# Pieces of two long filters, spread in another way over the four batches of a delta rule

## What is computed

```python
q = silu(dwconv(x @ q_w.T)); k = ...; v = ...          # 4 heads of 64 channels
beta = sigmoid(x @ b_w.T)
# delta rule, per head, in chunks of the sequence
inv = solve_triangular(eye + A, eye, lower=True)       # A = strictly lower part of (k*beta) @ k.T
u = inv @ v; w = inv @ kb
u_adj = u_i - w_i @ S; o_i = q_i @ S + attn @ u_adj; S = S + k_i.T @ u_adj
short, long_, wide = fir(v, 3 taps), fir(v, 31 taps), fir(v, 64 taps)   # causal, one filter a channel
gate_in = concat(x, stats(short), stats(long_), stats(wide), stats(delta_out), stats(v))
o = w0*short + w1*long_ + w2*wide + w3*delta_out + w4*v
```

## Time and profile before

| | |
|---|---|
| median of 3 runs | 709.68 us (709.62 to 709.91) |
| the profiled execution | 705.24 us |
| its span, first to last instruction | 703.4 us |
| busy, share of the span | PE 83%, PEld 61%, DVE 65%, ACT 40%, POOL 17% |
| mean granted clock of TensorE | 0.944 of full |

### The profile page before, as it was taken

How to read it: one execution, slowest core, us unless ns; L and a number is a source line. 1 busy time by engine, 2 the same in 40 slices (tenths; PEclk the granted TensorE clock), 3 DMA queues, 4 the chain that set the end, 5 groups by cost and what they waited for, 6 DMA issues and landing times. The chain is left out here.

```text
span 703.4 us, 16960 instructions
## 1 busy us (share of the span) xinstructions
PE 585.3 (83%) x7436; PEld 426.2 (61%) x7448; DVE 455.5 (65%) x890; ACT 282.8 (40%) x518; POOL 118.5 (17%) x102
## 2 busy tenths in 40 slices
PE   5868679899998999878696886599999767998984
PEld 2544466777767676776443545488888554555542
DVE  2963367857784786774818889664277774676674
ACT  1874634432453344323344253332323144554431
POOL 1001340250034006000011203434100020000000
PEclk9999899999999999998799998899999887999998
DMA  5501420340052004001510005400000000000001
GB/s 175 207 1 44 152 79 4 104 139 4 4 156 89 3 23 161 4 4 64 207 31 30 31 0 156 134 1 0 1 1 0 1 0 1 1 0 31 31 4 58
DMA packets 26537, 37.51 MB, mean 53 GB/s; under 512 B 4641, under 2 KB 13602, under 8 KB 26463
## 3 DMA queue, kind: packets, MB, share of 16 engines
q1 hardware_dynamic: 26463, 36.42, 16.0%
HBM read 34.31 MB, written 2.10 MB: 52 GB/s over the span
## 5 line engine op out<-in xcount | busy, mean ns | idle before, releaser
L298 DVE SCALAR_TENSOR_TENSOR arena<-bank,conv_w,arena 128x511 f32<-128x511 f32 (+2 forms) x72 | 53.2, 746 | 30.9 <-ACT arena L1070 15.5
L1448 POOL COPY arena<-v_win 128x256 f32<-128x256 f32 x32 | 21.1, 684 | 196.8 <-PE bank L732 196.8
L1898 ACT COPY arena<-bank 128x512 f32<-128x512 f32 x40 | 23.3, 584 | 57.1 <-PE bank L1701 36.8
L1701 PE MATMUL bank<-v_win,arena 128*128 128x256 f32 x192 | 45.6, 386 | 0.0
L2473 PE MATMUL bank<-v_win,arena 128*128 128x256 bf16 x288 | 36.5, 279 | 7.9 <-DVE arena L2560 6.9
L732 PE MATMUL bank<-arena 128*32 128x128 f32 x512 | 35.7, 409 | 8.1 <-ACT arena L1081 7.6
L1131 ACT COPY arena<-bank 128x512 f32<-128x512 f32 x40 | 21.6, 589 | 50.8 <-PE bank L854 50.8
L1086 ACT COPY arena<-bank 128x256 f32<-128x256 f32 x32 | 19.3, 602 | 53.9 <-PE bank L745 53.9
L1701 PEld LDWEIGHTS bank<-v_win,arena 128*128 128x128 f32 x192 | 37.1, 195 | 5.5 <-issue 0.4
L2473 PEld LDWEIGHTS bank<-v_win,arena 128*128 128x128 bf16 x288 | 28.4, 100 | 16.6 <-DVE arena L2560 7.9
L2463 PE MATMUL bank<-arena,v_win 128*128 128x512 bf16 x134 | 35.1, 390 | 3.7 <-DVE arena L2531 3.2
(11 more groups left out here) (275 smaller groups left out, 1355.4 us busy)
## 6 DMA issues: line engine op xcount, KB each, us to landing
arena<-in_toep_w SPq DMA_DIRECT2D x32, 256.0 KB, 3.0
arena<-in_toep_l SPq DMA_DIRECT2D x32, 256.0 KB, 3.7
arena<-in_xT SPq DMA_DIRECT2D x12, 512.0 KB, 4.6
arena<-in_x SPq DMA_DIRECT2D x4, 512.0 KB, 3.9
arena<-in_ctx SPq DMA_DIRECT2D x4, 512.0 KB, 4.4
out<-arena SPq DMA_DIRECT2D x4, 512.0 KB, 2.9
qkv_w<-in_qkv_wT SPq DMA_DIRECT2D x1, 768.0 KB, 5.4
v_win<-in_w_gateT SPq DMA_DIRECT2D x1, 768.0 KB, 4.9
```

The costliest lines, as they stand in the source:

```text
L298: return nc.vector.scalar_tensor_tensor(out=acc[:, j:L], in0=src[:, 0:L - j], scalar=conv_w[:, m, CONV_K - 1 - j:CONV_K - j], in1=acc[:, j:L],
L1701: i = mm(oo, src[:, k, f * P:(f + 1) * P], w[:, k, :], start=(k == 0), stop=(k == KT - 1 and f > 0))
L1898: nc.scalar.copy(dst(i), bank[RING_FIRST + n % RING].rearrange("p (t c) -> p t c", c=dst(i).shape[-1]))\
```

## The change

The recurrences of batches 0 and 1 get six pieces each in place of seven, that of batch 2 gets five, and pieces 25 to 28 go to the inverse of batch 3, one each at k = 2 to 5, where a batch with a successor has its projections. Their last turn stands where the next batch's `beta` would. The last recurrence keeps pieces 29 to 31. The work is the same; DVE's list does not change.

```diff
-        OPENING, PER_ROUND = 8, 7
-        pieces_of = lambda b: range(OPENING + b * PER_ROUND, min(OPENING + (b + 1) * PER_ROUND, NPIECE))
+        OPENING = 8
+        FIRST_OF, LAST_LEVELS = (8, 14, 20, 29, NPIECE), range(25, 29)
+        pieces_of = lambda b: range(FIRST_OF[b], LAST_LEVELS[0] if b == B - 2 else FIRST_OF[b + 1])
...
+                    if b == B - 1:
+                        for n in LAST_LEVELS:
+                            next_toep(n)
...
-                        pe.wait_ge(s2["fir_out"].sem, pieces_of(b)[0])
+                        pe.wait_ge(s2["fir_out"].sem, pieces_of(b - 1).stop if b else OPENING)
...
+                        else:
+                            if k == 2:
+                                pe.wait_ge(s2["attn_out"].sem, s2["attn_out"].at(b, 4))
+                            filter_piece(LAST_LEVELS[k - 2], first=(k == 2))
                         products_w(b, k, 0)
...
+                    else:
+                        to_tokens(LAST_LEVELS[-1])
                     corner(b, 0)
...
-                    if more:
+                    if last == 5:
                         filter_piece(piece[5])
 
                     state_part(b, 3)
-                    if more:
-                        filter_piece(piece[6])
                     updates(b, 3, more)
...
-                        to_tokens(piece[6])
+                        to_tokens(piece[last])
...
+                        if not more and k >= 2:
+                            filter_out(LAST_LEVELS[k - 2], first=(k == 2))
...
-                        copy_piece(piece[-1] + 1)
-                        copy_piece(piece[-1] + 2)
+                        for n in range(piece[-1] + 1, FIRST_OF[b + 1] + 2):
+                            copy_piece(n)
```

More of the change, by code:

```diff
@@ L974, in recurrence @@
                     piece = list(pieces_of(b))
+                    last = len(piece) - 1
                     if more:
@@ L1150, in inverse @@
                         beta_tanh(b + 1)
+                    else:
+                        tokens_out(LAST_LEVELS[-1])
                 def u_out(b, t):
@@ L1180, in recurrence @@
                         k_back_out(b + 1, 0, 1)
-                        filter_out(piece[5])
-                        filter_out(piece[6])
+                        for n in piece[5:]:
+                            filter_out(n)
                     else:
@@ L1187, in recurrence @@
                         cross_out(b + 1, 0)
-                        tokens_out(piece[6])
+                        tokens_out(piece[-1])
                         cross_out(b + 1, 1)
```

## The result

| | before | after |
|---|---|---|
| median of 4 runs each, same chip | 709.65 us (709.34 to 709.91) | 700.23 us (699.04 to 700.49) |
| ratio, 95% interval | | 0.9864 [0.9847, 0.9881] |
| the profiled execution | 705.24 us | 700.49 us |
| its span | 703.4 us | 698.7 us |

The account below looks back on a forecast made before the run. PE was taken to set the pace, with late code blocks and half clock in the last inverse. Recurrences -6.17 us and last inverse +1.6 us gave -4.6, so 709.68 became 705.1 us, range 701.8 to 707.8.

Parts of the forecast that it names:

- The recurrences: Recurrences of batches 0 to 2: removing pieces saves 1.50, 1.50 and 3.17 us, together 6.17 us.
- The Gram products: Gram products of batches 0 and 1: issue waits of 1.03 and 0.73 us, taken as staying in the sum.
- a rival from it for the worse alone: Gram products of batches 0 and 1: waits grow, each batch saves 1.0 us instead of 1.5; 706.1 us.
- The last inverse: Batch 3's inverse: four added pieces cost +1.6 us, the middle between -0.4 (none shows) and +3.6 (code blocks at batch 2's pace).
- Rival 2: Last inverse: levels run at batch 2's pace of code blocks, one in 4.62 us, +3.6 us; 707.1 us, chance 0.20.
- the inverse of batch 1: Batch 1's inverse: the forecast sum had no term for it.
- added its difference to the median: Whole kernel: median lies 4.4 us above the profiled execution, difference taken as unchanged, so -4.6 was applied to 709.68 us.
- Rival 1: Last inverse and Gram products: everything hidden and both Gram waits go, -8.3 us in all; 701.4 us, chance 0.13.
- Rival 3: Last inverse: each code block takes 5.29 us, +7.8 there, sum +1.6, a slower kernel; 711.3 us, chance 0.07.
- rival 4: Last recurrence at half clock: up to 3.9 us more could go; shifts each case by +-1.5 us; no chance of its own.

Follow-up runs that it names:

- the padded kernels: The kernel before with 64 or 128 instructions of unread 64x64 products added on PE in the opening; 0.9901 and 0.9924 of the kernel before.
- the two later comparisons: The changed kernel, unchanged, run again beside the kernel before, twice; 0.9891 (700.58 us against 707.67) and 0.9888 (699.85 us against 706.67).
- the control with 256: The kernel before with a whole block of 256 unread instructions (64 products of 64x64) added in the opening; 1.0051 of the kernel before.
- the pairs with equal padding: Kernel before and changed kernel, each with the same unread instructions in the opening: 0.9901 and 0.9918 with 64, 0.9924 and 0.992 with 128.
- two pieces: Against the changed kernel, two pieces instead of four in the last inverse, 7, 7 and 5 in the recurrences; 0.9915 of the kernel before.
- before again: The kernel before, unchanged, profiled and timed once more beside itself; 0.9979 of itself.
- removal alone: Against the changed kernel, pieces 25 to 28 left out altogether, nothing in the last inverse; 0.9855 of the kernel before, 697.81 us.

## Why the prediction was wrong

**The recurrences: right.** A clean recurrence with seven pieces takes 28.2 us, as the padded kernels show; after the change they are 26.7, 26.7 and 24.9. That is 1.5 + 1.5 + 3.3, where 1.50 + 1.50 + 3.17 were forecast.

**The Gram products: the first step that failed.** The sum took their two issue waits as staying, although had a price for them, and gave their going only to a rival. They went. The recurrence of batch 0 lost 2.7 and 2.0 us against the two profiles of before, that of batch 1 2.4: in the mean 1.7 us more than the pieces give. That these waits stand at borders of blocks is shown by the counts and the packets; the prediction had even said that the borders move by a piece's 64 instructions and drew a rival from it for the worse alone.

**The last inverse: the second step that failed, a right length from a wrong base.** The term was +1.6 us, on a base of 33.4. The changed stretch is 34.6 to 34.9 us, and the base is 33.5 in one profile and 35.9 in the other, so the measured term is +1.3 or -1.2, about nothing in the mean. But the pieces are not hidden. Against the same inverse without late blocks, 30.6 us, they cost 4.2 us: from level 2 to the end of `corner` 26.9 against 22.6 us (290.99 to 311.54 + 2.06 in the kernel with 64 instructions more). The prediction had 25.1 us for this without late code. Of the 1.8 us above it 0.6 are issue waits (0.26 and 0.38); the rest is spread over the levels (5.02 for 4.94) and the products behind them. It looked free since the base wasted 3 to 5 us. Rival 2's 29.1 us, a block each 4.62 us, did not come either: a block took 4.3.

**A term at nothing: the inverse of batch 1.** It takes 35.4, 35.5 and 34.5 us in the three profiles of the changed kernel against 34.47, since a block is late there in two of them (0.43 and 0.29 us, at different levels). That is +0.7 in the mean. The prediction had moved borders in mind, but not here.

**Summed up.** -4.6 as forecast, -1.7 for the Gram products, -1.6 for the inverse and +0.7 for batch 1's inverse give -7.2 us; stage 2 is 7.2 us shorter in the mean of the profiles (287.5, and 280.3 over three). The medians of the two later comparisons differ by 7.1 and 6.8 us. This is half as much again as forecast.

**The other 2 us.** The first comparison has 9.4 us. Its four executions of the kernel before have a median of 709.65 us, where the four later sets (11 to 29 executions each) have 706.7 to 707.7; the changed kernel has 700.2, 700.6 and 699.9. So the surplus lies on the side of the kernel before, in those four executions, and its cause stays open. The prediction, made against one execution 4.4 us under this median, added its difference to the median. That step did no harm: the two profiles of the kernel before differ by 3.0 us, 2.9 of them ahead of stage 2, where both kernels run the same code. What a single profile could not tell was how its last inverse and last recurrence share their half clock.

**The rivals.** Rival 1 came nearest in time (701.4), and half of its mechanism held, the waits in the Gram products; that everything is hidden in the last inverse did not. Rival 3, a slower kernel by late blocks, did not come; its mechanism was real but was in the kernel before. The clock (rival 4) moved 2.5 us in the base's last inverse and 1.7 us the other way in the recurrence behind it. The Trainium skill's page "Runtime: NRT & Kernel Launch", section "Instruction fetch mechanics", has blocks of 256 instructions, and the control with 256 and the places of all 36 waits bear that out. It has the cost of crossing a border as mostly hidden. By number of borders that holds, 36 waits at 681 of them; by time it fails here, since these few and the half clock behind them make most of the 7 us between good and bad borders in stage 2.

**What the change is worth.** The kernel before with 64 unread instructions is at 0.9901 [0.987, 0.9931], the changed kernel at 0.9864 to 0.9891. The later two comparisons of the changed kernel can't be told from it. Most of the gain is code that comes in time; moving pieces from the recurrences (6.3 us) to the last inverse (4.2 us) leaves at most 2 us, and in the pairs with equal padding nothing measurable. No kernel tried that does all the work was clearly faster than the changed one.

## What to carry to other kernels

Before costing a move of work, list the waits marked issue and count the instructions between them. When they are a block apart, look up when the packets of the instruction queue start, and ask what a shift of the borders would do, for the better as well as for the worse. A kernel with a few unread instructions more is the control without which a gain is put down to the wrong cause; check what the padding itself does to the time and the clock, and do not expect a whole block more to bring every wait back. Price a stretch against its clean length, not against one that carries a late block. And take a second profile of the kernel before, and compare stage by stage, before reading a gain off one pair of totals.

## What the runs showed of the hardware

- PE's code came in blocks of 256 instructions. In 18 profiles PE crossed no border of 681 sooner than 2.2 us after the packet of that block had started, and all 36 issue waits of over 0.2 us stand at such borders. In the late cases the packet started 1.0 to 4.0 us behind the border before. What sets that start was not settled.
- The rate of code is not all. Levels that ask for 272 instructions in 4.33 us ran without a wait with two placements of the borders (64 and 128 more) and lost 2 to 3 us in waits, and more to half clock, with two others that differ by a whole block (0 and 256 more). With four pieces in the levels each of the four placements tried had a wait.
- Nor is the place. At the border in batch 0's Gram products the wait was 1.03, 0.36, 1.30 and 0.91 us in four profiles, and absent in two others with the border at the same instruction (256 more, and two pieces). The longest wait at any border was 2.6 us.
- In the last inverse without a filling half clock followed in each of four profiles with late blocks, behind waits of 1.74, 1.11, 1.46 and 0.58 us (before, before again, 256 more, removal alone), and behind none in the three without a late block. 64 matmuls took 1.93 us for 1.16 there. With pieces in it the clock stayed at 1.00 behind waits of 1.12 and 1.62 us, as it did behind 2.0 and 2.6 us in the Gram products. So the fuller PE did keep the clock up; what it saved so was not measured apart.
